# Rows of 320 floats in place of 313 in the DRAM table of the edge build's parts

## The chip, the cores and the metric

One core of one Trainium2 chip runs the whole program. The time is that of the device in microseconds for one execution; lower is better. The profile is one execution recorded by the hardware profiler.

## The reference

The kernel computes four graph layers, one after the other, on 1250 nodes with 512 features and 40,000 weighted edges (`src`, `dst`; the edges are sorted by `dst`). Every layer is applied to the normalized and rectified `x` and added to it:

```python
h = jnp.maximum(_layernorm(x, axis=-1), 0.0)
x = x + layer(h, edges, ...)          # four times, with four layers
# layer 0: agg = segment_sum(x[src], ...), two linear maps, layer norm
# layer 1: attention of 8 heads along the edges, linear maps, layer norms
# layer 2: softmax weights of edge_weight per source, sums over edges both ways, linear maps
# layer 3: mean over the incoming edges, two linear maps, relu
```

All layers need sums over edges. The kernel makes them dense: a 1250 x 1250 matrix that counts the edges between two nodes, and another that sums their exponentiated weights. With these every sum over edges is a matrix product.

## The kernel before

**The edge build** (about 30 to 237 us of the trace). The edges lie in 320 chunks of 125. Two one-hot matrices, one by source and one by destination, are multiplied on TensorE (L556). The destinations are cut into 80 windows of 16 nodes (10 tiles of 128 nodes, 8 windows each); the sources into four quarters of 313 (the last has 311 real ones). The stationary operand has 128 columns: 4 parts x 4 quarters x 8 destinations, where part 0 counts edges and parts 1 to 3 are the three bf16 pieces of the edge weight. So a product leaves, in each of 128 partitions, one row of 313 sums, and the partition number is (part, quarter, destination).

VectorE writes the one-hot matrices of the sources: L1098 the fixed ones (8 for a group of two windows), L1116 those of a loop whose count depends on the data. A group of two windows fills four banks of PSUM. ScalarE copies each window (two halves of 8 destinations, 626 columns) into a buffer in SBUF (L1437). There are three buffers, each of one group; before ScalarE may fill one again, it waits until the stores of the group three back have landed. SP stores a window with two DMAs in `move_window` (L340), one for each half: 128 rows of 313 floats from SBUF into the DRAM table `edge_parts`, declared in L102 with the shape (4 parts, 4 quarters, 1280 destinations, QUART = 313), at 8 neighbouring destinations in each of the 16 (part, quarter) regions. Once a tile has its 8 windows, and 4 windows later, `load_counts` reads part 0 of the tile back, three quarters with one DMA (L349) and the last with another (L351), and ScalarE adds up the degrees (L1429).

The semaphores make the order: SP waits for ScalarE's copy (`win_free`) before L340, ScalarE for the landing of stores (`win_moved`), TensorE for ScalarE's copy before it reuses the PSUM banks, VectorE for TensorE's use of a one-hot matrix. SP issues all DMAs of the kernel, in program order, on one queue.

**After the build** TensorE goes on with the aggregation of layer 0 (L589), which needs the last window's banks and the counts. Later the table is read twice more. During the attention (some 470 to 650 us) `load_parts` reads parts 1 to 3 of a quarter of a tile (L358), GpSimd adds them (L1651, L1653), and `store_sum` writes the sum into another table, `edge_sums`, with rows of 1250 floats (L365). All of `edge_sums` is read at 782 us (L422). At 942 us L440 reads part 0 of `edge_parts` again, a quarter with each of four DMAs, for the last layer (first used by L873 in `turn_c`).

Of the kernel before, what the change touches and what calls it, by code (L numbers as in the profile page):

```python
# [18 lines left out]
F32 = mybir.dt.float32  # L19
# [4 lines left out]
P = 128  # L24
N, D, E = 1250, 512, 40000
T = -(-N // P)
# [16 lines left out]
QUART = -(-N // 4)  # L43
LASTQ = N - 3 * QUART
HOT = QUART + 1
NQ = 4 * QUART
KEY = 512.0
PS_N = 2
# [31 lines left out]
def constants():  # L80
# [13 lines left out]
    k1[:, NK1:NK1 + 2 * NW] = np.arange(2 * NW) * KEY  # L94
    iota = np.broadcast_to(np.arange(HOT, dtype=np.float16), (P, HOT)).copy()
    return k1, k2, iota


def build(nc, A, out):
    dram_w = nc.dram_tensor("edge_sums", (T * P, N), F32, kind="Internal").ap()  # L100

    dram_p = nc.dram_tensor("edge_parts", (4, 4, T * P, QUART), F32, kind="Internal").ap()  # L102

    with ExitStack() as ctx:
        def sb(name, shape, dt=F32):
# [63 lines left out]
        SLOTS = 2 * BASES + GH  # L169
        src_oh = HT[0:EC, 0:SLOTS * HOT // 2].bitcast(BF16).rearrange("p (s n) -> p s n", n=HOT)  # L170
        epsI = BC[:, 1536:1536 + P]
# [8 lines left out]
        winI = BC[0:1, 1200:1200 + NG * VALUES].bitcast(I32)  # L180
        iota = BC[:, W0 + 3 * NC // 2:W0 + 3 * NC // 2 + HOT // 2].bitcast(F16)

# [1547 lines left out]
```

How the kernel before makes its waits and increments, by code:

```python
        @block.sync  # L302
# [30 lines left out]
            def move_window(w):  # L333
                g, half = divmod(w, GH // 2)
                b = winbuf[g % WB_N][:, half * 2 * QUART:(half + 1) * 2 * QUART]
                moved = sem("win_moved%d" % (g % WB_N))
                sp.wait_ge(sem("win_free"), w + 1)
                for h in range(2):
                    d0 = w * WIN + h * SUB
                    sp.dma_start(dram_p.rearrange("k q d n -> (k q) d n")[:, d0:d0 + SUB, :],
                                 b[:, h * QUART:(h + 1) * QUART]).then_inc(moved, 16)
# [1 line left out]
            def load_counts(t):  # L343
                for q in range(WB_N):
                    sp.wait_ge(sem("win_moved%d" % q), moved((t + 1) * OCT * 2 // GH - 1, q))
                if t >= 2:
                    sp.wait_ge(sem("c_in%d" % (t % 2)), 32 * (t // 2))
                c = dram_p[0, :, t * P:(t + 1) * P, :].rearrange("q p n -> p q n")
                sp.dma_start(cd[:, t, 0:3 * QUART].rearrange("p (q n) -> p q n", q=3), c[:, 0:3, :])\
                    .then_inc(sem("c_in%d" % (t % 2)), 16)
                sp.dma_start(cd[:, t, 3 * QUART:N], c[:, 3, 0:LASTQ]).then_inc(sem("c_in%d" % (t % 2)), 16)
# [21 lines left out]
            sp.wait_ge(sem("base_used"), BASES * NG)
            sp.dma_start(wb4, A["L0_W2T"].rearrange("(k p) o -> p k o", p=P)).then_inc(sem("l0_w_in"), 16)
# [2 lines left out]
            load_x(0, 7, "x_in")
            sp.wait_ge(sem("hw"), T)
            sp.wait_ge(sem("l0_w_in"), 32)
```

## Time and profile before

| | |
|---|---|
| three runs | 1161.2, 1165.61, 1166.24 us |
| median | 1165.61 us |
| the profiled execution | 1164.15 us, of which 1162.2 us from the first to the last instruction |
| mean granted TensorE clock | 0.973 |
| TensorE busy | 1066.3 us (92%) |
| VectorE, ScalarE, GpSimd busy | 598.7, 446.0, 157.7 us |
| DMA | 92.62 MB on SP's queue, 27.2% of 16 engines' time |

In the views quoted below "busy" is the time in which an engine had an instruction at work. "DMA share" is the mean busy share of the core's 16 DMA engines in a stretch (rounding and packets that cross an edge can carry it a little over 1), GB/s what they moved in it; the one divided by the other is the rate that the engines would have at full share. Of a DMA instruction the trace has the time that SP takes to issue it, and the time from issue to landing.

### The profile page before, as it was taken

To read this page: it belongs to the slowest core of one execution; us is meant where nothing else is said; L and a number is where in the kernel's file an instruction comes from. 1 tells how busy PE (TensorE), PEld (TensorE's weight loads), DVE (VectorE), ACT (ScalarE), POOL (GpSimd) and SP (SyncE) were. 2 spreads that over 40 slices of the span, in tenths; PEclk is the share of its full clock that TensorE was granted. 3 is DMA by queue.
4 is the path that set the end of the run, shared out by engine and by line. 5 is a ranking of instruction groups with operands and counts; after the bars stand their busy time and mean duration, and the time that the engine had idled before them with its cause. 6 is when DMAs were issued, how large, how long until landed. Compare 5 with 4: busy or idle time off the path is not lost.

```text
span 1162.2 us, 16827 instructions
## 1 busy us (share of the span) xinstructions
PE 1066.3 (92%) x5904; PEld 693.0 (60%) x5904; DVE 598.7 (52%) x1743; ACT 446.0 (38%) x762; POOL 157.7 (14%) x182
## 2 busy tenths in 40 slices
PE   6988877789998999899999999999989997999998
PEld 3455555545544455577777777775546896555443
DVE  6889998820386101465665665664447335400132
ACT  5601454420345300555655655652336414500000
POOL 0000000000024100233333100004637012000000
PEclk9999988889999999899999999999999998999999
DMA  5003699990010010454544200017001050100011
GB/s 165 1 0 89 172 249 245 239 262 17 0 62 0 1 37 1 157 145 139 148 139 142 93 1 2 1 40 279 1 0 46 1 195 28 37 1 1 9 40 40
DMA packets 73041, 93.63 MB, mean 81 GB/s; under 512 B 7113, under 2 KB 63120, under 8 KB 72966
## 3 DMA queue, kind: packets, MB, share of 16 engines
q1 hardware_dynamic: 72966, 92.62, 27.2%
q8 instruction: 48, 0.79, 0.3%
q14 instruction: 27, 0.22, 0.1%
HBM read 58.00 MB, written 34.60 MB: 80 GB/s over the span
## 4 chain that ended last, share of the span: by engine, by line
PE 76%; DVE 7%; issue 5%; DMA 5%; ACT 4%; SPq 2%; DVEq 0%; ACTq 0%
PE PS L787 8%; PE PS L589 8%; PE PS L770 7%; PE PS L928 7%; PE PS L742 7%; PE PS L963 6%; PE PS L556 6%; PE PS L713 5%; PE PS L612 5%; DMA edge_parts<-X 5%; PE PS L528 2%; DVE R L1233 2%; PE PS L699 2%; PE PS L890 2%; PE PS L910 2%
## 5 line engine op out<-in xcount | busy, mean ns | idle before, releaser
L556 PE MATMUL PS<-HT,R 125*128 125x313 bf16 x636 | 139.5, 358 | 35.2 <-ACT X L1437 15.9
L1222 DVE CUSTOM_DVE_ANT_0 HT<-PS,CD 128x1250 f32<-128x1250 f32 (+1 forms) x80 | 116.3, 1454 | 68.9 <-issue 68.9
L556 PEld LDWEIGHTS PS<-HT,R 125*128 x636 | 98.3, 172 | 76.5 <-issue 56.1
L770 PE MATMUL PS<-K,HT 128*128 128x128 f32 (+2 forms) x800 | 112.4, 280 | 15.1 <-DVE R L1233 14.4
L1527 ACT COPY R<-PS 128x512 f32<-128x512 f32 (+1 forms) x120 | 64.8, 574 | 122.7 <-PE PS L770 120.7
L1547 ACT ACTIVATE HT<-HT,soft 128x1250 f32<-128x1250 f32 (+1 forms) x80 | 107.1, 1338 | 10.2 <-DVE soft L1225 3.1
L770 PEld LDWEIGHTS PS<-K,HT 128*128 128x128 f32 (+2 forms) x800 | 84.0, 140 | 43.2 <-DVE R L1233 23.6
L1116 DVE TENSOR_SCALAR HT<-BC,HT 125x314 bf16<-125x314 f16 x316 | 91.8, 361 | 19.5 <-PE PS L556 17.6
L742 PE MATMUL PS<-R 64*128 64x512 f32 (+3 forms) x480 | 97.0, 536 | 3.1 <-DVE soft L1222 3.1
L787 PE MATMUL PS<-R 128*64 128x128 f32 (+2 forms) x1600 | 94.2, 273 | 0.0
L1437 ACT COPY X<-PS 128x626 f32<-128x626 f32 x80 | 52.5, 687 | 108.8 <-PE PS L556 75.9
L589 PE MATMUL PS<-CD,H 128*128 128x512 f32 (+2 forms) x240 | 87.2, 526 | 3.4 <-issue 3.4
L787 PEld LDWEIGHTS PS<-R 128*64 128x64 f32 (+1 forms) x1600 | 84.8, 137 | 6.4 <-issue 5.8
L1233 DVE COPY R<-PS 128x512 f32<-128x512 f32 (+1 forms) x80 | 54.3, 678 | 65.2 <-PE PS L770 65.2
L928 PE MATMUL PS<-R,H 128*128 128x512 f32 (+2 forms) x240 | 85.2, 513 | 0.0
L742 PEld LDWEIGHTS PS<-R 64*128 64x128 f32 (+1 forms) x480 | 61.8, 187 | 31.4 <-issue 22.7
L1343 DVE SCALAR_TENSOR_TENSOR R<-PS,invdeg,BC 128x512 f32<-128x512 f32 (+1 forms) x10 | 7.5, 750 | 133.0 <-PE PS L963 133.0
L589 PEld LDWEIGHTS PS<-CD,H 128*128 128x128 f32 (+1 forms) x240 | 46.6, 195 | 44.1 <-issue 43.9
L1098 DVE TENSOR_SCALAR HT<-BC 125x314 bf16<-125x314 f16 x320 | 71.5, 300 | 0.0
L713 PE MATMUL PS<-HT,R 128*128 128x512 f32 (+1 forms) x192 | 67.4, 513 | 0.8 <-ACT HT L1477 0.8
L928 PEld LDWEIGHTS PS<-R,H 128*128 128x128 f32 (+1 forms) x240 | 45.0, 189 | 38.7 <-issue 38.4
L1405 ACT ACTIVATE rs<-mv,gate 128x1 f32<-128x1 f32 x70 | 20.6, 294 | 111.7 <-DVE mv L1077 111.7
(220 smaller groups left out, 1389.2 us busy)
## 6 DMA issues: line engine op xcount, KB each, us to landing
edge_parts<-X SPq DMA_DIRECT2D x160, 156.5 KB, 4.9
R<-edge_parts SPq DMA_DIRECT2D x60, 156.5 KB, 2.4
CD<-edge_sums SPq DMA_DIRECT2D x1, 6250.0 KB, 20.9
CD<-edge_parts SPq DMA_DIRECT2D x10, 469.5 KB, 4.7
BC<-edge_parts SPq DMA_DIRECT2D x30, 156.5 KB, 2.4
CD<-edge_parts SPq DMA_DIRECT2D x3, 1565.0 KB, 11.0
edge_sums<-R SPq DMA_DIRECT2D x20, 156.5 KB, 2.9
R<-edge_parts SPq DMA_DIRECT2D x18, 155.5 KB, 2.4
```

The lines of the kernel that those rows point to most:

```text
L556: return mm(bank(b0 + h, QUART), stat, hot, start=first, stop=True, skip_group_check=True)
L589: i = mm(bank(b0 + j, sn), H[0:rows(t), t, f * P:(f + 1) * P], cd[0:rows(t), t, s0:s0 + sn], start=t == 0, stop=t == T - 1, skip_group_che ...
L713: i = mm(bank(5 * m + j, sn), wqk[p % 2][:, m, k, :], ht[:, k, s0:s0 + sn], start=k == 0, stop=k == KF - 1)
L742: i = mm(PS[0:n, a * N + s0:a * N + s0 + sn], qT[a * DK:(a + 1) * DK, p, t * P:t * P + n], kT[a * DK:(a + 1) * DK, p, s0:s0 + sn], start=T ...
L770: m = nc.tensor.transpose(PS[0:rows(j), o:o + n], Pb[u % 2][a][0:n, j * P:j * P + rows(j)], ident[0:n, 0:n])
L787: m = mm(PS[a * DK:(a + 1) * DK, o:o + n], V[0:rows(j), j, (2 * p + a) * DK:(2 * p + a + 1) * DK], PT[c % RING][0:rows(j), (2 * jj + a) * ...
L928: i = mm(bank(3 * (f % 2) + j, sn), H[0:rows(t), t, f * P:(f + 1) * P], cs[0:rows(t), t, s0:s0 + sn], start=t == 0, stop=t == T - 1)
L1098: ve.tensor_scalar(src_oh[:, base_slot(w, q * GH + h), :], iota[0:EC, :], base_key[:, q, v:v + 1], None, ALU.is_equal).then_inc(sem("base_ ...
L1116: ve.tensor_scalar(late_oh[:, h, :], iota[0:EC, :], key_base[0:EC, v:v + 1], key[:, late_chunk(d[h], m)], ALU.add, ALU.is_equal)\
L1222: ve.tensor_tensor_reduce(Pb[s][a][0:n], PS[0:n, a * N:(a + 1) * N], cd[0:n, t, :], 1.0, -3e38, ALU.add, ALU.max, soft[0:n, s, a:a + 1]).t ...
L1233: ve.tensor_copy(PT[c % RING].rearrange("p (j n) -> p j n", j=4)[:, :, 0:n], bank(6 + c % 2).rearrange("p (j n) -> p j n", j=4)[:, :, 0:n])\
L1547: sc.activation(Pb[s][a][0:n], Pb[s][a][0:n], ACT.Exp, bias=soft[0:n, s, 2 + a:3 + a], accum_out=zsum[0:n, z + a:z + a + 1]).then_inc(sem( ...
```

## The change

The table `edge_parts` is declared with rows of 320 floats, and all the transfers get a view of it that ends each row at 313. Every transfer, its number of rows and its bytes stay the same; the distance between rows in DRAM becomes 1280 bytes, that between two (part, quarter) regions 1280 x 1280 bytes. The second table, `edge_sums`, is as it was.

```diff
@@ -43,6 +43,7 @@
 QUART = -(-N // 4)
 LASTQ = N - 3 * QUART
 HOT = QUART + 1
+PITCH = 320
 NQ = 4 * QUART
 KEY = 512.0
 PS_N = 2
@@ -99,7 +100,7 @@
 def build(nc, A, out):
     dram_w = nc.dram_tensor("edge_sums", (T * P, N), F32, kind="Internal").ap()
 
-    dram_p = nc.dram_tensor("edge_parts", (4, 4, T * P, QUART), F32, kind="Internal").ap()
+    dram_p = nc.dram_tensor("edge_parts", (4, 4, T * P, PITCH), F32, kind="Internal").ap()[:, :, :, 0:QUART]
```

## Rows read from the trace of the kernel before

**Rows 1.** The page: busy tenths in 40 slices of the span, and GB/s
```profile
DVE  6889998820386101465665665664447335400132
...
DMA  5003699990010010454544200017001050100011
GB/s 165 1 0 89 172 249 245 239 262 17 0 62 0 1 37 1 157 145 139 148 139 142 93 1 2 1 40 279 1 0 46 1 195 28 37 1 1 9 40 40
```

**Rows 2.** Windows table: stretch, its us, busy by engine, granted clock, DMA share, GB/s
```profile
91.00:104.00 13.00, 11.53 (x49) 7.57 (x48) 12.49 (x49) 2.49 (x4) 0.00 (x0) 1.00 0.34 99
104.00:117.00 13.00, 10.91 (x47) 7.28 (x47) 11.80 (x48) 2.62 (x5) 0.00 (x0) 0.88 0.35 101
...
137.00:232.00 95.00, 71.31 (x354) 53.21 (x355) 84.83 (x364) 50.30 (x80) 0.00 (x0) 0.87 0.97 241
```

**Rows 3.** Waits, 137 to 232 us: engine, line, releaser, us in total, times, longest
```profile
ACT X L1437 <- DMA edge_parts<-X: 30.5, 19, 3.1
...
PE PS L556 <- ACT X L1437: 12.5, 8, 2.7
...
DVE HT L1116 <- PE PS L556: 10.0, 10, 2.7
```

**Rows 4.** Chain of waits, 137 to 232 us, shares by line
```profile
by line: DMA edge_parts<-X 57.2%; ACT X L1437 12.6%; PE PS L556 9.8%; SPq L340 9.8%; issue 3.7%; DVE HT L1098 2.6%; ACT H L1423 2.1%; DVE HT L1116 1.4%; SPq L351 0.6%; ACTq L1435 0.1%; DVEq L1112 0.1%; DVEq L1116 0.1%; SPq L349 0.0%
```

**Rows 5.** Line L340, 60 to 120 us, then 137 to 232 us
```profile
L340 SPq DMA_DIRECT2D edge_parts<-X x20: 517/599/619, 91.7 to 119.5; - x20
...
DMA to landing us min/median/max: 2.5/3.1/3.6
...
L340 SPq DMA_DIRECT2D edge_parts<-X x116: 517/600/1568, 136.6 to 231.6; - x116
...
DMA to landing us min/median/max: 2.8/5.2/7.2
```

**Rows 6.** Waits of SP's queue, 137 to 232 us
```profile
SPq L340 <- ACT X L1437: 14.6, 24, 1.4
```

**Rows 7.** SP's timeline (start us, us) near 504 us, and windows of it
```profile
503.44 1.27 SPq L358 DMA_DIRECT2D R<-edge_parts  x3
504.76 0.43 SPq L365 DMA_DIRECT2D edge_sums<-BC  x1
...
505.00:505.25 0.25, 0.25 (x5) 0.25 (x6) 0.25 (x1) 0.25 (x2) 0.00 (x0) 1.00 1.07 371
...
506.75:507.00 0.25, 0.25 (x9) 0.25 (x7) 0.25 (x1) 0.25 (x1) 0.00 (x0) 1.00 0.61 215
```

**Rows 8.** Windows table: reload of edge_sums (L422), reload of edge_parts (L440)
```profile
783.00:806.00 23.00, 21.18 (x146) 12.36 (x147) 8.85 (x23) 6.68 (x14) 7.17 (x10) 1.00 1.00 370
...
941.00:963.00 22.00, 22.00 (x200) 22.00 (x199) 10.18 (x50) 6.02 (x19) 5.87 (x12) 1.00 0.87 292
```

**Rows 9.** Chain of waits, 228 to 300 us, a piece near its start
```profile
234.41 3.35 issue
```

**Rows 10.** Chain of waits, 470 to 700 us, shares by line
```profile
by line: PE PS L787 27.4%; PE PS L742 27.4%; PE PS L770 27.2%; issue 12.1%; DVE R L1233 8.5%; PE PS L799 2.5%; DVE soft L1225 0.3%; DVE soft L1222 0.2%; DVE HT L1222 0.1%
```

**Rows 11.** Line L440, and a piece of the chain of 930 to 975 us
```profile
L440 SPq DMA_DIRECT2D CD<-edge_parts x4: 377/2092/4137, 941.6 to 946.3; - x4
...
DMA to landing us min/median/max: 7.1/13.4/16.6
...
968.12 1.27 PE PS L873 x10
```

**Rows 12.** The page: packets of the whole execution
```profile
DMA packets 73041, 93.63 MB, mean 81 GB/s; under 512 B 7113, under 2 KB 63120, under 8 KB 72966
```

## The prediction

> **What bounds the kernel now.** I read the page's slices first. The DMA row stands at 9 tenths in the sixth to the ninth slice (145 to 261 us) with 239 to 262 GB/s beside it, while VectorE is at 8 or 9 tenths up to the eighth [rows 1]. This is the edge build: TensorE builds one window of the edge matrix after another, ScalarE copies each out of PSUM (L1437), SP stores it in the table `edge_parts` with two DMAs (L340), and once per tile of eight windows SP loads a part of the table back (L349, L351). The windows table shows two regimes in it. From 91 to 117 us the DMA share is 0.34 to 0.35; from 137 to 232 us it is 0.97 at 241 GB/s [rows 2]. In the second one the chain of waits runs over the store for 57% of the time [rows 4], and the waits say how: a copy can't start before the stores of three groups back have left its buffer (30.5 us of ScalarE), TensorE then waits for the copy (12.5 us), and VectorE waits for TensorE (10.0 us) [rows 3]. A store lands 3.1 us after its issue in the light stretch and 5.2 us in the heavy one [rows 5]. So this stretch is the only one in which the speed of the table's transfers sets the end.
>
> How much is there to gain or lose? VectorE is busy for 84.8 of the 95 us [rows 2], so with free transfers the stretch can shrink by 10.2 us. SP comes next: 95 us less its waits of 14.6 us for ScalarE [rows 6] are 80.4 us of issuing, under VectorE's 84.8. At the end of the stretch TensorE waits another 3.35 us before the aggregation begins, behind the last copies, which wait for stores as well [rows 9]; I allow 2 of it. The ceiling of any gain is thus about 12 us. For a loss there is no such cover: at a share of 0.97 whatever the transfers take longer is paid in full.
>
> **The change part by part.** The table's row becomes 1280 bytes apart instead of 1252; 1252 bytes of it (1244 in the last quarter) are moved as before. No instruction is added, removed or moved, and no wait. What can change is the price of a transfer, through two facts about addresses. First, a row began at any multiple of 4 bytes and now begins at a multiple of 256 (its end stays odd). Second, the 16 regions into which one L340 writes (4 parts by 4 quarters) were 1280 x 1252 = 1,602,560 bytes apart, 1565 times 1 KiB, and are now 1,638,400 bytes apart, 25 times 64 KiB: all 16 streams of a store now agree in the low 16 bits of their addresses, where before they were scattered.
>
> *The issue on SP.* An L340 takes 600 ns at the median; three L358 take 1.27 us and an L365 0.43 us, though the former read rows that lie back to back and the latter writes rows 5000 bytes apart [rows 5, 7]. So whether rows touch costs SP nothing, and I take 0, with 0.1 us per issue as the outer bound: 116 issues would then put SP at 92 us, still inside 95. The page counts 63120 packets under 2 KB [rows 12]; one packet per row of the table's and the sums' transfers makes 51,200 of them (160 stores, 120 part loads, 40 sum stores of 128 rows, 10 count loads of 512, one reload of 5120). Had a store's eight touching rows gone out as one run, 20,480 would be missing and nothing else in the kernel could fill the place. So no merging is lost.
>
> *The start of a row.* The trace has misaligned rows of the same size in other places. At 504.76 us SP issues the store of a sum, 128 rows of 1252 bytes at a pitch of 5000, behind three loads from the table [rows 7]. If the engines take them in the order of issue (the trace doesn't name a packet's transfer), its packets are the last: 506.75 to 507.00 us shows 215 GB/s at a share of 0.61, 352 GB/s for a full share. The loads ahead of it show 371 at 1.07, 347 for a full share [rows 7]. Both are misaligned, and both are close to the 370 GB/s at 1.00 of the 5000-byte rows read at 783 us [rows 8]. The scattered stores of L340 reach only 99/0.34 = 291 GB/s in the light stretch and 241/0.97 = 248 in the heavy one, loads included [rows 2]. So what makes L340 dear is something that it doesn't share with the sum's store, and misalignment is shared. That speaks for a cost near nothing of the start of a row, at least for one transfer alone; crowded, no row isolates it.
>
> The Trainium skill says the contrary for the start of a row (DMA: Bandwidth & Descriptors, How a descriptor splits into AXI transactions): a transaction begins on a 256-byte boundary, so that a row that starts past one also moves the bytes below it. By that rule a row here costs 43.5 beats on average and 40 after the change, 8% less, and an estimate from the page is 94.2 us less 7.5 us for the stretch. The 352 GB/s of the misaligned store speaks against it.
>
> *The spread of the regions.* A tile is 16 stores of 0.160 MB and 0.64 MB of loads, 3.20 MB; at 248 GB/s that is 12.9 us for a full share, of which the loads are 1.9 us at the 292/0.87 = 336 GB/s of the reload [rows 8]. The stores have 11.0 us for 2.56 MB: 233 GB/s. The excess over the 336 is what the spread, the direction and the crowding cost, 3.4 us of a tile and some 24 us of the 7.25 tiles. The new spacing may take from it or add to it; the trace shows no store at another spacing. I take 0, because the old spacing was no special one and the new one is odd in units of 64 KiB, so higher bits of the addresses still differ.
>
> *Loads elsewhere.* The part loads of 470 to 650 us are waited for by GpSimd alone, and the chain of that time holds TensorE and VectorE, no DMA [rows 10]; the sums are wanted at 782 us. The reload of L440 is issued from 941.6 to 946.3 us and lands within 16.6 us, by 963 us; TensorE's first use is about 968 us [rows 11]. It hides as long as it isn't a quarter slower. Both at 0.
>
> **Sum.** 1164.15 us (profiled) + 0 + 0 + 0. The median of the three runs is 1165.6, 1.5 above it. I forecast 1165.0, and 1160 to 1171 for this case alone, which holds changes of the stretch's transfer rate of up to about 5% either way (5% of 95 us is 4.8 us).
>
> **The rivals.**
> *A, aligned rows make crowded stores cheaper.* For it: only in the heavy stretch do the stores fall to 233 GB/s, and the sum's store that I hold against it was alone. If a quarter of the 3.4 us goes, a tile takes 12.04 instead of 12.9 us of share, and the stretch gives back 95 x 0.067 = 6.3 us; if half goes (11.2 us), the transfers are faster than VectorE's 84.8/7.25 = 11.7 us per tile and the whole 10 us come. I put it at 8 us: 1157.6. Next in line are VectorE (L1098, L1116) and SP.
> *B, nothing measurable* is the forecast: the excess is crowding and spread.
> *C, slower: the 16 streams of a store, equal in their low 16 bits, get in each other's way.* They run side by side through eight rows each. For it: spread stores already cost 291 against 352 GB/s, 17%, where nothing crowds them. Against it: the spacing is no power of two. Another 17% on the stores is 11.0/0.83 - 11.0 = 2.3 us per tile, 16 us in all: 1181; half of that, which I take as its size, gives 1173.5. It decides from the first per cent on, since the share is 0.97. The Trainium skill (DMA: Bandwidth & Descriptors, Latency and other measured facts) has a rule of this kind: row pitches of 2 MiB and more cost a fifth to a half of the rate, 512 KiB did not; it calls the mechanism an inference. The new spacing of 1.56 MiB is between these and an odd multiple of 64 KiB, and no run here shows which side it falls on.
> *D, the change doesn't reach the transfers* (rows still merged or split otherwise) gives the time of B, and is counted there.
>
> **How the numbers follow.** B 0.45, A 0.33, C 0.22. A reaches from 1154 to 1160, C from 1169 to 1181. The range of 1155 to 1174 leaves out about 0.06 below and 0.09 above, and some noise. A measurement of this kernel can tell about 0.5%, 5.8 us, from no change. Faster by over 0.5%: 0.33 (A, but for its weakest part, and the best part of B); within: 0.45; slower: 0.22.
>
> **What would show it.** In the profile after: the DMA share and GB/s of 137 us to the last window (B: 241 at 0.97; A: 260 or more, share below 0.95; C: under 225 at full share); L340's landing in the heavy stretch (B 5.2 us; A 4 or less; C 6 and over); ScalarE's 30.5 us behind stores; VectorE's busy time stays 84.8 us in all cases, its idle time tells the gain. L340's issue stays at 600 ns. The light stretch tells A from C by itself, without a queue: 291 GB/s for a full share now. I am wrong if the landing there moves while the issue doesn't, or if the time moves outside the build.

## The result, and the profile after

The changed kernel takes 1150.2 us (median of four runs, 1147.9 to 1153.1) against 1165.9 us: a ratio of 0.9865, 95% interval 0.9839 to 0.9891. That is 1.35% faster, where no change was forecast, and below the range of 1155 to 1174 us. The profiled execution spans 1145.9 us after 1162.2.

The page of the changed kernel, to be held against [rows 1] (busy tenths in 40 slices, GB/s; a slice is 28.6 us here):

```profile
DVE  6889999910685010565666656655456235400122
...
DMA  5002588870010010545454200026001060100010
GB/s 167 1 0 84 160 267 270 266 243 1 1 62 1 1 37 1 183 137 152 141 154 121 89 1 1 2 83 241 1 1 46 1 224 1 37 1 1 9 46 35
```

In the sixth to the ninth slice the DMA engines are less busy (8, 8, 8, 7 for four 9s) and move more (266 to 270 GB/s in three of them). The rest is the same picture. The windows table of the changed kernel, and then that of the kernel before for the same stretches (stretch, its us, busy by engine, granted clock, DMA share, GB/s):

```profile
91.00:104.00 13.00, 11.59 (x48) 7.66 (x48) 12.59 (x50) 2.56 (x4) 0.00 (x0) 1.00 0.34 99
137.00:222.00 85.00, 69.74 (x341) 52.84 (x341) 80.48 (x344) 49.06 (x79) 0.00 (x0) 0.86 0.87 265
145.00:205.00 60.00, 48.96 (x240) 37.13 (x240) 56.20 (x241) 35.12 (x57) 0.00 (x0) 0.86 0.88 268
```

```profile
145.00:205.00 60.00, 44.97 (x228) 33.77 (x227) 53.33 (x228) 31.11 (x50) 0.00 (x0) 0.89 0.99 246
137.00:222.00 85.00, 63.69 (x316) 47.40 (x316) 76.41 (x327) 46.24 (x74) 0.00 (x0) 0.88 0.96 240
```

From 145 to 205 us the engines would move 246/0.99 = 248 GB/s at full share before and 268/0.88 = 305 after: the same transfers cost 19% less. I call this quotient the **full-share rate** below; it is the number that tells the kernels apart. VectorE fills 80.5 of 85 us, where it had 76.4.

The stores and the waits of the changed kernel, which answer to [rows 3] and [rows 5] (line L341 from 60 to 120 us, then over the whole build; waits from 137 to 222 us):

```profile
L341 SPq DMA_DIRECT2D edge_parts<-X x19: 517/599/620, 92.2 to 119.4; - x19
...
DMA to landing us min/median/max: 2.4/2.6/3.8
...
L341 SPq DMA_DIRECT2D edge_parts<-X x160: 517/600/2030, 92.2 to 232.2; - x160
...
DMA to landing us min/median/max: 2.4/2.8/4.9
```

```profile
ACT X L1438 <- PE PS L557: 35.7, 23, 4.3
...
PE PS L557 <- DVE HT L1099: 14.9, 7, 2.4
DVE HT L1117 <- PE PS L557: 4.0, 6, 1.3
ACT X L1438 <- DMA edge_parts<-X: 0.9, 1, 0.9
```

ScalarE's 30.5 us behind stores [rows 3], 27.2 of them in this stretch, are 0.9 us. What TensorE waits for now is VectorE. The chain of waits of the changed kernel from 137 to 222 us has no DMA left, where the store had 57.2% of it [rows 4], and the aggregation (L590) follows the last copies at 228 us:

```profile
by line: PE PS L557 37.8%; DVE HT L1099 30.2%; DVE HT L1117 16.8%; issue 10.2%; DVEq L251 2.2%; DVEq L1113 1.7%; DVEq L1117 1.2%
```

```profile
223.41 3.28 PE PS L557 x14
226.71 1.27 ACT X L1438 x2
228.07 72.11 PE PS L590 x205
```

**Where the 16.3 us of the two traces lie**, by the first and last matmul of each stage:

| stage | before | after | saved so far |
|---|---|---|---|
| the build's first matmul (L556) | 59.7 | 60.3 | -0.6 |
| the aggregation's first matmul (L589) | 237.8 | 228.1 | 9.7 |
| the aggregation's last matmul | 324.6 | 312.0 | 12.6 |
| the last of the projections (L699) | 470.7 | 458.1 | 12.6 |
| the attention's first L787 | 489.2 | 474.4 | 14.8 |
| the attention's last L787 | 790.2 | 775.5 | 14.7 |
| the last L637 | 887.5 | 871.2 | 16.3 |
| the last output DMA | 1159.5 | 1143.2 | 16.3 |

The build gives 10.3 us. The rest comes in three steps (2.9, 2.2 and 1.6 us) at places that the change doesn't touch, and the granted clock of TensorE goes with them: the instructions are the same, and before it was lower (in the third step 0.94 to 0.96 for 1.00). Kernel before, then changed kernel, at the start of the aggregation and of the attention:

```profile
237.00:247.00 10.00, 9.24 (x18) 4.72 (x19) 0.52 (x2) 2.00 (x4) 0.00 (x0) 0.67 0.65 176
474.00:484.00 10.00, 7.14 (x27) 4.88 (x28) 5.44 (x13) 4.46 (x7) 4.33 (x6) 0.66 0.84 275
```

```profile
228.00:238.00 10.00, 9.93 (x28) 5.38 (x29) 2.59 (x12) 1.34 (x2) 0.00 (x0) 1.00 0.69 203
461.50:470.00 8.50, 4.54 (x28) 3.23 (x28) 6.07 (x16) 5.50 (x9) 4.34 (x6) 1.00 0.81 272
```

The build of before ended with TensorE waiting [rows 9], and the clock was at the lower level for part of the next 10 us; after, it went from one work into the other. The first of the three steps recurs: over all traces of this study the aggregation takes 83.9 or 84.0 us in each kernel whose build is not held up by its stores (eleven of them, the changed one included), and 83.9 to 87.0 us in the nine whose build is held up; three of these nine have 83.9 or 84.0 as well. The two later ones are not tied as firmly. The second step (the gap from the projections to the attention, 18.5 us before and 16.3 after) is there in nine of the eleven and in three of the nine; the third (97.3 and 95.7 us from L787 to L637) in five of the eleven and in one of the nine. e0_padded below, with the same stores as the changed kernel, has the first two and little of the third, and ends 12.4 us before the kernel before, not 16.3.

### The profile page after: what moved, and what is told of

The parts are those of the page before. It is cut to its first block, busy times and chain, and to the rows that moved or that the text cites. A ratio compares the mean times of both kernels' runs of the same rounds, so it can differ in the third digit from the quotient of the medians.

```text
span 1145.9 us, 16827 instructions
## 1 busy us (share of the span) xinstructions
PE 1059.4 (92%) x5904; PEld 690.6 (60%) x5904; DVE 598.9 (52%) x1743; ACT 446.6 (39%) x762; POOL 157.9 (14%) x182
## 4 chain that ended last, share of the span: by engine, by line
PE 78%; DVE 10%; issue 5%; ACT 3%; SPq 1%; DMA 1%; DVEq 0%; ACTq 0%
PE PS L557 8%; PE PS L788 8%; PE PS L771 7%; PE PS L590 7%; PE PS L929 7%; PE PS L743 7%; PE PS L964 6%; PE PS L714 5%; PE PS L613 5%; DVE HT L1099 2%; PE PS L529 2%; DVE R L1234 2%; PE PS L700 2%; PE PS L891 2%; PE PS L911 2%
## 5 line engine op out<-in xcount | busy, mean ns | idle before, releaser
L557 PE MATMUL PS<-HT,R 125*128 125x313 bf16 x636 | 140.2, 360 | 26.5 <-DVE HT L1099 14.9
L590 PE MATMUL PS<-CD,H 128*128 128x512 f32 (+2 forms) x240 | 84.3, 513 | 1.0 <-ACT X L1438 1.0
L590 PEld LDWEIGHTS PS<-CD,H 128*128 128x128 f32 (+1 forms) x240 | 45.4, 189 | 39.8 <-issue 39.7
```

The source lines that it names most:

```text
L557: return mm(bank(b0 + h, QUART), stat, hot, start=first, stop=True, skip_group_check=True)
L590: i = mm(bank(b0 + j, sn), H[0:rows(t), t, f * P:(f + 1) * P], cd[0:rows(t), t, s0:s0 + sn], start=t == 0, stop=t == T - 1, skip_group_che ...
```

## The experiments

All kernels below differ from the changed one in one more thing, so that a wait against a register can't see a negative value. e0_padded has only that:

```diff
-                     v[VALUES * k + GH].with_bounds(...))
+                     smax(v[VALUES * k + GH], 0).with_bounds(...))
```

> The changed kernel with one register operation more per group and engine: the bound of the data-dependent loop is taken as max(value, 0). All the kernels below have it too, so this is the one to hold them against. Every theory: 1150 us (ratio 0.985 to 0.990), stores land in 2.8 us at the median, DMA share 0.86 to 0.90 from 145 to 205 us. If the operation costs something, some 0.1 us for each of 40 groups, 4 us at most.

Measured: 1150.7 us, ratio 0.990 (0.987 to 0.993); median landing from 137 us on 2.8 us; 266 GB/s at 0.86 (309). Its build is 1.4 us longer in the trace than the changed kernel's; in the times the operation can't be seen. Its window of 145 to 205 us:

```profile
145.00:205.00 60.00, 49.25 (x240) 37.05 (x240) 55.95 (x239) 34.99 (x57) 0.00 (x0) 0.86 0.86 266
```

The layout is the changed kernel's, so 305 and 309 GB/s also show how far one layout's rate differs between two traces. Each ratio below is against the kernel before as measured in the same round, whose median was 1162.2 to 1167.9 us; compare the ratios rather than the times.

Three theories were on the table: R, the spacing of the 16 regions; A, a row's start on a multiple of 256; S, that two rows share a piece of memory. The experiments e1 to e3, e5, e6, e8, e9, e12 to e15 and e17 declare the table by three numbers, here those of e2, and every transfer keeps its rows and bytes:

```diff
-PITCH = 320
+PITCH, REGION, START = 320, 411200, 0        # floats
...
+    dram_p = nc.dram_tensor("edge_parts", (4, 4, REGION), F32, kind="Internal").ap()[:, :, START:START + T * P * PITCH]\
+        .rearrange("k q (d n) -> k q d n", n=PITCH)[:, :, :, 0:QUART]
```

**Regions or rows?** e1 has 313, 409600, 0; e2 has 320, 411200, 0; e3 has 320, 425984, 1.

> Rows of 1252 bytes back to back as before, but the 16 regions 1,638,400 bytes apart as after. If the spacing of the regions did it (theory R): like the changed kernel, 1150 us, heavy-stretch landing 2.8 us. If the start of a row does it, be it that it lies on a 256-byte multiple (theory A) or that two rows share no small piece of memory (theory S): like the kernel before, 1165 us, landing 5.2 us at a share of 0.97.

> Rows 1280 bytes apart as after, the regions 1,644,800 bytes apart (1285 rows, scattered over 64 KiB as before). Theory R: 1165 us, landing 5.2 us. Theories A and S: 1150 us, landing 2.8 us.

> Rows 1280 bytes apart, each starting 4 bytes past a multiple of 256 (regions 26 x 64 KiB apart). It still ends at 1256 of its 1280 bytes, so that two rows share no piece of 24 bytes or more around their border. Theory A (the start must lie on a multiple): 1165 us, landing 5.2 us. Theory S (rows must not share a piece): 1150 us, landing 2.8 us. Theory R: 1150 us.

Windows of 145 to 205 us, of e1, e2 and e3 in this order, each from its own trace:

```profile
145.00:205.00 60.00, 46.06 (x238) 35.72 (x238) 54.95 (x235) 31.88 (x51) 0.00 (x0) 0.89 0.97 254
```

```profile
145.00:205.00 60.00, 48.25 (x240) 36.86 (x240) 56.82 (x243) 35.67 (x58) 0.00 (x0) 0.86 0.88 268
```

```profile
145.00:205.00 60.00, 48.91 (x240) 36.79 (x240) 56.79 (x242) 35.90 (x58) 0.00 (x0) 0.86 0.87 264
```

e1 takes 1160.4 us (ratio 0.998, 0.995 to 1.000) with a landing of 4.8 us; e2 1152.2 us (0.992, 0.990 to 0.994) with 2.9 us; e3 1149.3 us (0.990, 0.987 to 0.993) with 3.0 us. So the rows do it. The spacing alone gives a full-share rate of 262 for 248 and an aggregation that begins 3 us earlier, a small share at the edge of what the times can tell. Theory A falls with e3: a start 4 bytes past the multiple is as good as one on it. S stands.

**How large is the piece?** e12 starts at 28 bytes, e9 at 32, e5 at 64 (START 7, 8, 16; pitch 320; REGION 425984 as in e3).

> Rows 1280 bytes apart, each starting 64 bytes past a multiple of 256. The last bytes of a row and the first of the next lie in the same 256-byte piece (and the same 128-byte piece) but in different 64-byte pieces. Theory S64 (what costs is two rows in one piece of 64 bytes or less): 1150 us, heavy-stretch landing 2.8 us. Theory S256 (a piece of 128 or 256 bytes): 1163 us, landing 5 us.

> As the last, but each row starts 32 bytes past a multiple of 256: its last 4 bytes share a 64-byte piece with the first 32 bytes of the next row, and no 32-byte piece. If the piece is one of 64 bytes: 1163 us and 5 us to land. If it is one of 32 bytes or less: 1150 us and 2.8 us. If it is 128 or more: slow here and with the start at 64.

> Rows 1280 bytes apart, each starting 28 bytes past a multiple of 256, one float before the start of e9_start_32. The row ends exactly on a multiple of 256, so it lies in 5 pieces of 256 bytes; with the start at 32 it lies in 6. Theory N (the number of 256-byte pieces that a row touches): fast as e0_padded, 1150 us, heavy-stretch landing 2.8 to 3.0 us, ScalarE behind stores for under 4 us. Theory D (the distance from an aligned start, growing with it): between e3_start_4 and e9_start_32, landing 3.5 to 4.2 us.

e12, then e9, then e5, 145 to 205 us:

```profile
145.00:205.00 60.00, 48.16 (x237) 36.53 (x236) 55.47 (x237) 34.53 (x55) 0.00 (x0) 0.83 0.86 261
```

```profile
145.00:205.00 60.00, 47.82 (x240) 36.20 (x240) 56.01 (x240) 34.29 (x55) 0.00 (x0) 0.89 0.95 265
```

```profile
145.00:205.00 60.00, 47.12 (x236) 35.30 (x236) 54.95 (x235) 32.59 (x53) 0.00 (x0) 0.89 0.95 258
```

One float between e12 and e9 takes the full-share rate from 303 to 279, the landing from 2.8 to 4.2 us and ScalarE's wait behind stores from none to 10.5 us (137 to 222 us); e5 has 272, 4.4 us and 14.9 us. The times are 1148.7, 1158.6 and 1155.9 us (0.989, 0.994, 0.994). A start at 32 moves the row's last 4 bytes over a multiple of 256. So the piece is larger than 64 bytes (e5 shares none of 64), and two readings are left: pieces that a row *touches* (theory N, 5 or 6 of 256 bytes), or pieces that two rows *share*.

**Touched or shared?** e13 and e14 have a pitch of 384 and start at 128 and at 64 bytes, e15 a pitch of 320 and a start at 128. REGION is 507904, 507904 and 425984.

> Rows 1536 bytes apart, each starting 128 bytes past a multiple of 256: 6 pieces of 256 bytes per row, 10 of 128 (as in the changed kernel), and no piece of any size is shared by two rows. Theory N: as slow as e5_start_64, landing 4.3 us, some 1155 us. If what costs is that two rows share a piece (theory S, with pieces of 128 or 256 bytes), or the number of 128-byte pieces: fast, landing 2.9 us, 1150 us.

> Rows 1536 bytes apart, starting 64 bytes past a multiple of 256: 11 pieces of 128 bytes per row (10 with the start at 128), no piece of any size shared by two rows. Theory C128 (the number of 128-byte pieces that a row touches, 10 fast and 11 slow): like e5_start_64, landing 4.4 us, DMA share of 145 to 205 us 0.95, some 1155 us. Theory S (a piece shared by two rows): fast, landing 2.9 us, share 0.88, 1151 us.

> Rows 1280 bytes apart, starting 128 bytes past a multiple of 256: 10 pieces of 128 bytes, none shared by two rows; the end of a row and the start of the next share a piece of 256 bytes. Theory C128: fast, landing 2.9 us, share 0.88. Theory S with pieces of 256 bytes: slow, 4.4 us and 0.95. Theory S with pieces of 128: fast.

e13, e14, e15, 145 to 205 us:

```profile
145.00:205.00 60.00, 48.82 (x240) 36.80 (x240) 56.43 (x241) 35.42 (x57) 0.00 (x0) 0.86 0.88 267
```

```profile
145.00:205.00 60.00, 48.98 (x240) 37.06 (x240) 55.66 (x239) 35.40 (x57) 0.00 (x0) 0.86 0.88 267
```

```profile
145.00:205.00 60.00, 48.61 (x240) 36.88 (x240) 55.90 (x237) 34.82 (x56) 0.00 (x0) 0.86 0.89 268
```

All three are fast: 303, 303 and 301 GB/s, landing 2.9 us, no wait of ScalarE behind a store; 1152.8, 1153.0 and 1147.8 us (0.992, 0.992, 0.988). e13 touches six pieces of 256 bytes and e14 eleven of 128 at no cost, so neither count matters. e15 shares a piece of 256 bytes between rows, none of 128, at no cost. With e5 slow this leaves **a piece of 128 bytes that two rows share while both are being stored**. The traces part the two groups clearly, one trace for each kernel: of all layouts in this order of the table, those below included, the fast ones have 301 GB/s or more, the slow ones 279 or less. The times alone do it narrowly: ratios of 0.987 to 0.992 against 0.994 to 1.001.

**Pieces written in part, and the mixture.** e4 gives each buffer row 320 floats and stores all of them; e6 has a pitch of 328 floats, e17 one of 381 (START 0, REGION 1280 rows each).

```diff
...
-                    sp.dma_start(dram_p.rearrange("k q d n -> (k q) d n")[:, d0:d0 + SUB, :],
-                                 b[:, h * QUART:(h + 1) * QUART]).then_inc(moved, 16)
+                    sp.dma_start(dram_f.rearrange("k q d n -> (k q) d n")[:, d0:d0 + SUB, :],
+                                 b[:, h * PITCH:(h + 1) * PITCH]).then_inc(moved, 16)
...
```

> The table of the changed kernel, but the stores write all 320 floats of a row (the 7 beyond 313 are what lies in the buffer, and nobody reads them), so that no piece of 32 bytes or more is written in part. Theory N: no gain over e0_padded, 2% more bytes: 1150 us, landing 2.8 us. If pieces that are written in part cost by themselves: landing 2.5 us or less and a share under 0.85, but no shorter build, since VectorE bounds it then.

> Rows 1312 bytes apart: the start steps through all multiples of 32 bytes within 256, 60 bytes lie between two rows. 5.88 pieces of 256 bytes per row as in the kernel before, 3.5 of 512 bytes (before 3.44; 3.0 in all kernels with a fixed start). Theory N alone: landing 4.3 us as with the starts at 32 and 64. If the rows of before are slower than those because their starts differ from row to row: landing 5 us and 1160 us or more. If it is because rows touch: 4.3 us.

> Rows 1524 bytes apart: the start steps through all multiples of 4 within 256 as in the kernel before, but 272 bytes lie between two rows, so that no piece of up to 256 bytes is shared. If sharing a 128-byte piece is all that costs (theory S128): fast, landing 2.9 us, share of 145 to 205 us 0.88 at 267 GB/s. If starts that differ from row to row cost by themselves (theory V): slow, 4.5 us or more, 0.95 to 0.99.

e4: 271 GB/s at 0.87 (311), landing 2.8 us, 1152.2 us (0.992): that pieces are written in part costs next to nothing. e17: 265 at 0.87 (305), landing 3.2 us, ScalarE 5.4 us behind stores, 1152.3 us (0.987): starts that step through all phases cost next to nothing as long as nothing is shared. e6 is slow, 252 at 0.97 (260), landing 4.6 us, 1158.6 us (0.996), though only half of its rows share a 128-byte piece with the next; that it is no better than the starts at 32 and 64, where all do, I can't explain.

**At which distance in time?** e10 puts the table in another order, in which the next row in memory belongs to the next tile and is stored 8 windows later; e11 has the same instructions and the old order. In both, the count loads are one DMA for each quarter and the reload for the last layer is 40 DMAs. From e11 to e10:

```diff
-    dram_p = nc.dram_tensor("edge_parts", (4, 4, T, WIN, SUB, QUART), F32, kind="Internal").ap()
+    dram_s = nc.dram_tensor("edge_parts", (4, 4, SUB, WIN, T, QUART), F32, kind="Internal").ap()
+    dram_p = dram_s.rearrange("k q s a t n -> k q t a s n")
```

e16 is e10 with rows of 320 floats, e18 is e16 with a start at 64 bytes, so that all rows share a 128-byte piece with one stored some 12 us away.

```diff
-    dram_s = nc.dram_tensor("edge_parts", (4, 4, SUB, WIN, T, QUART), F32, kind="Internal").ap()
+    dram_s = nc.dram_tensor("edge_parts", (4, 4, SUB, WIN, T, 320), F32, kind="Internal").ap()[:, :, :, :, :, 0:QUART]   # e16
+    dram_s = nc.dram_tensor("edge_parts", (4, 4, SUB * WIN * T * 320 + 16384), F32, kind="Internal").ap()[:, :, 16:16 + SUB * WIN * T * 320]\
+        .rearrange("k q (s a t n) -> k q s a t n", s=SUB, a=WIN, t=T)[:, :, :, :, :, 0:QUART]                            # e18
```

> Rows back to back at 1252 bytes as before, but in an order in which touching rows belong to the same window of neighbouring tiles, and are stored 8 windows (some 12 us) apart. Loads take one DMA per quarter and tile, as in e11_together, so the two are compared with each other, not with the rest. Theory H (two rows that share a piece disturb each other while both are in flight): fast, stores land in 3 us in the heavy stretch, the aggregation begins some 8 us earlier than in e11_together. Theory P (a piece that is written in part costs, whoever has the rest): slow like e11_together, landing 5 us.

> The control of e10_apart: the same instructions, the table in its order of before (rows back to back in the order of destinations). Both theories: landing 5 us in the heavy stretch and the build as long as before, plus up to 1 us per tile for two more DMAs on SP; the reload for the last layer is 40 DMAs and may cost some us at the end, in both.

> e10_apart (touching rows are stored 8 windows apart) with rows of 1280 in place of 1252 bytes, starting on multiples of 256. If the slowness of e10_apart is that of its rows (C128, or shared pieces that cost at any distance in time): fast, landing 3 us, share 0.88 and ScalarE no longer behind stores. If it came from the scattered order of its rows: as slow as e10_apart, landing 5 us at a share of 1.00; then e10_apart says nothing on rows.

> The order of e16_apart_320 (neighbours in memory are stored 8 windows apart), rows 1280 bytes apart but starting at 64: each row shares a 128-byte piece with one that is stored some 12 us earlier or later. If two writes to one piece only disturb each other in flight (theory H): as fast as e16_apart_320, landing 2.3 us, share 0.87 at 286 GB/s, 1147 us. If a shared piece costs at any distance in time: slow as e10_apart, 5 us at 1.00.

e10, e11, e16, e18, 145 to 205 us:

```profile
145.00:205.00 60.00, 44.92 (x221) 33.12 (x220) 51.80 (x221) 31.16 (x50) 0.00 (x0) 0.86 1.00 240
```

```profile
145.00:205.00 60.00, 46.99 (x228) 34.98 (x228) 54.10 (x231) 30.76 (x51) 0.00 (x0) 0.80 0.99 247
```

```profile
145.00:205.00 60.00, 52.27 (x257) 38.92 (x258) 59.64 (x258) 36.73 (x59) 0.00 (x0) 0.95 0.87 286
```

```profile
145.00:205.00 60.00, 46.30 (x228) 34.54 (x227) 54.38 (x233) 31.51 (x50) 0.00 (x0) 0.83 0.79 238
```

The times are 1161.6 us (0.998), 1163.1 (1.001), 1146.7 (0.986, 0.983 to 0.989) and 1160.5 (0.995). e18's own stores are cheap: a full-share rate of 301 and a landing of 2.6 us, though every row shares a piece. Its build is long for another reason, which its store line shows beside that of e16 (e18 first, with ScalarE's wait behind stores; 137 to 222 us):

```profile
L343 SPq DMA_DIRECT2D edge_parts<-X x101: 517/601/1968, 137.0 to 222.0; - x101
...
DMA to landing us min/median/max: 2.5/2.6/4.6
...
ACT X L1440 <- DMA edge_parts<-X: 17.3, 7, 5.1
```

```profile
L342 SPq DMA_DIRECT2D edge_parts<-X x119: 319/452/2040, 137.0 to 221.7; - x119
...
DMA to landing us min/median/max: 1.8/2.3/3.8
```

SP issues a store in 601 ns and, per tile, 16 of these and four loads of 0.6 us with their gaps, some 13 us in all; it waits for ScalarE for only 6.4 of 95 us (137 to 232 us), so it bounds the build itself. ScalarE's 17.3 us are then a wait for stores that were issued late, since they land within 2.6 us of their issue. In e16 the regions follow one another at the same step as a region's eight rows, the 128 rows are one run of equal steps, and an issue takes 452 ns.

By e18, sharing costs nothing where the other row is stored some 12 us away, at the share of 0.79 that SP leaves it; no run shows this at a full share. e10 speaks against it: it lands in 5.1 us at a full share (its control e11 in 4.6 us) though nothing that it shares is in flight together, and e16, the same order with rows of 1280 bytes, is fast. The two differ also in the step between the rows of a store (200,320 and 204,800 bytes). e10 is behind e16 already in the light stretch; e10, then e16:

```profile
91.00:104.00 13.00, 11.46 (x48) 7.55 (x48) 12.50 (x49) 2.10 (x4) 0.00 (x0) 1.00 0.34 99
91.00:104.00 13.00, 11.68 (x49) 7.69 (x48) 12.55 (x50) 2.56 (x4) 0.00 (x0) 1.00 0.28 99
```

That is 291 against 354 GB/s for a full share, and a landing of 2.6 against 1.9 us (60 to 104 us). All stores of this stretch belong to the first tile, and in this order no row that touches theirs has been stored yet. So at least this part of the difference isn't one of two writes that meet, and it points at the step. No run changed the step alone, and what makes e10 slow isn't settled.

**The spacing of the regions at its strongest.** e8 has 320, 1048576, 0.

> The changed kernel's rows, the 16 regions exactly 4 MiB apart. This is rival C of the prediction at its strongest: 16 streams that agree in 22 bits of their addresses. If such streams get in each other's way: landing well over 3 us in the heavy stretch, 1175 us or more. If not: 1151 us as e0_padded, and the rival was empty.

Stores of e8, 137 to 222 us, and its window of 145 to 205 us:

```profile
L343 SPq DMA_DIRECT2D edge_parts<-X x68: 517/600/1263, 136.8 to 216.6; - x68
...
DMA to landing us min/median/max: 4.3/8.7/13.8
```

```profile
145.00:205.00 60.00, 34.64 (x144) 23.15 (x144) 35.79 (x151) 22.42 (x37) 0.00 (x0) 0.71 1.00 164
```

1213.9 us, a ratio of 1.044 (1.040 to 1.047): rival C was a real mechanism at another spacing. The transfers cost nearly twice (164 for 305 GB/s), and the aggregation begins at 293 us. The Trainium skill (DMA: Bandwidth & Descriptors, Latency and other measured facts) has half the rate at a pitch of 4 MiB; this case agrees, with 164 for 305 GB/s at 4 MiB between regions of eight rows. At 1.56 MiB, 25 times 64 KiB, nothing of it is seen: e2, with scattered regions, and e0_padded, with these, have 305 and 309.

## Why the prediction was wrong, point by point

- **What bounds the build** was right: the stores were on the chain, and when they got cheaper VectorE came next. For this change the ceiling fitted: 10.2 us in the stretch and 2 at its end were allowed, the build gave 10.3 in the profile. As a limit of the build it was low: e16's is 14.8 us shorter than before (163.3 us from its first matmul to the aggregation, for 178.1).
- **The start of a row** is the step that failed: it put everything that the rows do at nothing, and the build gave 10.3 us, with a full-share rate of 305 for 248 GB/s. It held the sum's store, a misaligned one at 352 GB/s [rows 7], against the 291 and 248 of the table's stores [rows 2], and concluded that rows were innocent because misalignment was common to both. Misalignment is innocent, in truth (e3, e12, e13, e14, e15). But the two differ in a second property of rows, which the step passed over: the sum's rows lie 5000 bytes apart, the table's touch. The section said itself that a row read for one transfer alone doesn't show the crowded case; it should have kept the whole excess open. The 352 GB/s was a poor yardstick besides: of the quarters of a microsecond in which the three loads and this store move, and in which the share is above 0.5, it is the best. Two between them have 132 and 228 GB/s for a full share:

```profile
505.75:506.00 0.25, 0.25 (x8) 0.25 (x6) 0.25 (x1) 0.23 (x1) 0.00 (x0) 1.00 1.06 140
506.00:506.25 0.25, 0.25 (x10) 0.25 (x8) 0.25 (x1) 0.25 (x1) 0.00 (x0) 1.00 0.90 205
```

Over all quarters from 504.25 to 507.50 us, which hold the three loads and the store whole, it is 276 GB/s. What the store has by itself isn't known, since the trace doesn't name a packet's transfer. The 291 of the light stretch is a mean over whole transfers, so the two weren't like quantities, neither here nor in the 17% that rival C took from them.
- **The spread of the regions** was given the 3.4 us per tile. It had another owner. Of the difference of 248 to 305 GB/s the spacing has at most the step to 262 (e1), and nothing where rows don't share (e2). What the fast kernels lack to the 336 of the loads is about 9%. Most of this is again the place of the rows: e16, whose 128 rows are one run of equal steps of 204,800 bytes, reaches 286/0.87 = 329.
- **The light stretch** was read wrongly as well. Its share and GB/s didn't move (0.34 and 99 both times, [rows 2]), only the landing did, from 3.1 to 2.6 us. So the 291 GB/s there is not a sign of shared pieces, and the test that I named, A from C by that quotient, would have told nothing; the landing would.
- **Rival A** had the right sign, the right place and the right next bound, and its best case (10 us) came true. Its reason, aligned starts, didn't: it was right by luck. The rule of the Trainium skill (DMA: Bandwidth & Descriptors, How a descriptor splits into AXI transactions), by which a row that starts past a 256-byte boundary costs more beats, would have given 7.5 us for this change, by the prediction's estimate. By it e13 and e15, which start at 128 and so take 44 beats for 40, should have a rate some 9% lower than with a start at 0, an estimate from the same rule of the Trainium skill. They don't: 303 and 301 GB/s against 305 to 309. The reload of L440, whose rows began anywhere before and on a multiple of 256 after, ran at 292 GB/s and a share of 0.87 both times. Here the measurement decides against the estimate.
- **Rival C** was empty at this spacing; at 4 MiB the kernel takes 52 us more than the kernel before.
- **The issue on SP** (600 ns), **the loads** (the reload lands in 13.4 us at the median, [rows 11], as after) and **the sums by GpSimd** were right at nothing.
- **The clock** wasn't in the sum. The changed kernel's build ends without a long wait of TensorE, the granted clock of the next 10 us is 1.00 for 0.67, and the aggregation takes 2.9 us less. The two later steps I take in part for variation between executions, since kernels whose builds are equally fast have either value (e13 and e14 have a gap of 18.4 us before the attention, e15 16.3); nothing was run to show it.
- **The range** ended 10.6 us below the median of before, on the most that the build alone can give less a little; the build gave that most, and the clock and the other executions more.

**The shortest build.** e16_apart_320 has the lowest median, 1146.7 us (1143.9 to 1146.9), with VectorE at 59.6 of 60 us and an aggregation that begins at 223.9 us in place of 228.1. Its ratio to the kernel before, 0.986 (0.983 to 0.989), doesn't part it from that of the changed kernel, 0.9865, which was measured in other runs, and of the 4.2 us 1.3 are left at the end of its trace. So its build is shorter; that the kernel is faster isn't shown.

## What to carry to other kernels

Lay a DRAM table that is stored in rows out so that neighbouring rows of one store, or of stores in flight together, leave no 128-byte piece in common: it takes a gap with a multiple of 128 bytes in it or at its edge (at a pitch of 1280 bytes a start at 0, 4, 28 or 128 does, one at 32 or 64 doesn't), an aligned start is not needed, and the unused end need not be written. Whether neighbours that are stored far apart may share a piece is open (e18 says yes, e10 doesn't fit). Where the rows of a store can be one run of equal steps, try that as well (e16). When a row of the trace is used to clear a suspect, list every property in which it differs from the accused, not only the one in question, and compare rates over whole transfers. And where a stage's own chain runs through its stores at a full DMA share, treat their excess over the best transfer of the trace as open on both sides.

## What the runs showed of the hardware that was not expected

- Stores of 128 rows of 1252 bytes under load: a full-share rate of 301 to 311 GB/s where rows share no 128-byte piece (nine layouts of the ordinary order), 248 to 279 where they do. A shared piece of 256 bytes alone costs nothing (301).
- The loads of the same rows didn't move with the change: 292 GB/s with a share of 0.87 [rows 8] and a landing of 13.4 us in both kernels.
- The time from issue to landing moved by 0.5 us in a stretch in which busy share and GB/s stayed as they were.
- A store whose 128 rows are one run of equal steps is issued in 440 to 452 ns (e10, e16), one in 16 runs of eight in 600 ns. In the light stretch e16's lands in 1.9 us and has a full-share rate of 354 GB/s, against 2.6 us and 291 in the changed kernel; e10's lands in 2.6 us with 291, so the equal steps alone don't do it.
- 16 streams exactly 4 MiB apart halve the rate (164 GB/s).
